# A three-attention transformer kernel: read-out of values and denominators into full rows by VectorE, the key mask carried as a row of the keys' stacks, and other places for the splitting steps

## The reference

```
layer 0:  h = LN(x)*(1+sc)+sh;  q,k,v = h @ qkv_W, rope on halves of 64;  x += g * (softmax(qk/sqrt8, block mask 128x128) v) @ Wo
          h = LN(x)*..+..;      q = h @ cq, k,v = ctx @ ck, cv;          x += g * (softmax(qk/sqrt8, key mask 77) v) @ co
          x += g * (gelu(LN(x)*..+.. @ W1 + b1) @ W2 + b2)
layer 1:  q from LN(x), k,v from LN(ctx), both modulated;               out = x + (softmax(qk/sqrt8) v) @ Wp + bp
```

## Time and profile before

| | us |
|---|---|
| median of 3 runs (1298.3 to 1306.19) | 1305.03 |
| profiled execution | 1309.05 |
| its span, first to last instruction | 1307.3 |
| PE busy | 1182.8 (90%) |
| POOL busy | 898.4 (69%) |
| ACT busy | 887.2 (68%) |
| DVE busy | 736.2 (56%) |
| 16 DMA engines, queue of SP | 44.2% |

### The profile page before, as it was taken

How to read it: one execution, slowest core, us unless ns; L and a number is a source line. 1 busy time by engine, 2 the same in 40 slices (tenths; PEclk the granted TensorE clock), 3 DMA queues, 4 the chain that set the end, 5 groups by cost and what they waited for, 6 DMA issues and landing times.

```text
span 1307.3 us, 42601 instructions
## 1 busy us (share of the span) xinstructions
PE 1182.8 (90%) x16674; PEld 655.9 (50%) x16674; DVE 736.2 (56%) x1613; ACT 887.2 (68%) x1527; POOL 898.4 (69%) x1798
## 2 busy tenths in 40 slices
PE   2778889889888889999999999899998999999998
PEld 1434544444444444555555554344443566666666
DVE  5346677677666665666666664222224666666653
ACT  0235666666666556778778776777876788888765
POOL 0176786786787666777777752556877888888742
PEclk9889899999999899999999998899999899999888
DMA  3475455355354434564554550000023566666650
GB/s 98 117 165 101 74 97 100 71 98 101 69 100 85 85 56 79 84 105 79 88 97 78 97 98 15 1 1 1 4 49 53 85 114 112 117 117 117 109 98 28
DMA packets 147256, 105.84 MB, mean 81 GB/s; under 512 B 25049, under 2 KB 146802, under 8 KB 147058
## 3 DMA queue, kind: packets, MB, share of 16 engines
q1 hardware_dynamic: 147058, 103.12, 44.2%
HBM read 9.08 MB, written 4.19 MB: 10 GB/s over the span
## 4 chain that ended last, share of the span: by engine, by line
PE 59%; POOL 17%; ACT 9%; issue 8%; SPq 2%; DMA 2%; DVE 1%; POOLq 0%; ACTq 0%
PE ps_po L546 10%; PE ps_st L525 6%; PE ps_nat L491 5%; PE ps_pj L438 5%; PE ps_pj L416 4%; PE ps_pj L421 4%; ACT p L798 4%; PE ps_st L558 4%; PE ps_po L567 4%; PE ps_pj L381 4%; PE ps_nat L499 3%; POOL ht L906 3%; POOL ht L901 2%; PE ps_pj L429 2%; POOL ot L862 2%
## 5 line engine op out<-in xcount | busy, mean ns | idle before, releaser
L628 DVE TENSOR_REDUCE negmax<-ps_nat 128x8 f32<-128x616 f32 (+1 forms) x384 | 361.0, 940 | 196.2 <-PE ps_nat L491 109.5
L798 ACT ACTIVATE p<-ps_st 128x1024 f32<-128x1024 f32 (+1 forms) x256 | 260.5, 1018 | 200.5 <-PE ps_st L525 198.3
L546 PE MATMUL ps_po<-p,vz 77*32 77x128 f32 (+1 forms) x6144 | 256.7, 287 | 2.5 <-DVE mt L636 1.1
L862 POOL TENSOR_TENSOR ot<-vv,den 128x256 f32<-128x256 f32 x192 | 139.4, 726 | 150.1 <-ACT den L786 150.0
L798 ACT ACTIVATE p<-ps_st,key_bias 77x1024 f32<-77x1024 f32 x128 | 141.8, 1108 | 70.5 <-PE ps_st L525 70.5
L546 PEld LDWEIGHTS ps_po<-p,vz 77*32 77x32 f32 (+1 forms) x6144 | 149.5, 112 | 41.1 <-issue 4.8
L525 PE MATMUL ps_st<-stacks 64*77 64x128 bf16 (+1 forms) x3072 | 158.3, 224 | 7.6 <-ACT p L798 6.6
L491 PE MATMUL ps_nat<-stacks 64*128 64x77 bf16 (+1 forms) x3072 | 134.9, 210 | 4.8 <-DMA stacks<-parts 3.3
L491 PEld LDWEIGHTS ps_nat<-stacks 64*128 64x128 bf16 x3072 | 78.3, 97 | 116.1 <-issue 101.7
L874 POOL TENSOR_TENSOR whole<-whole,parts 128x512 f32<-128x512 f32 x96 | 98.6, 1027 | 54.4 <-ACT parts L733 54.3
L525 PEld LDWEIGHTS ps_st<-stacks 64*77 64x77 bf16 (+1 forms) x3072 | 104.7, 110 | 49.4 <-issue 28.0
(11 more groups left out here) (138 smaller groups left out, 2144.9 us busy)
## 6 DMA issues: line engine op xcount, KB each, us to landing
stacks<-parts SPq DMA_DIRECT2D x512, 128.0 KB, 3.2
stacks<-parts SPq DMA_DIRECT2D x256, 77.0 KB, 2.6
p<-in_x_dram SPq DMA_DIRECT2D x16, 256.0 KB
out_dram<-part SPq DMA_DIRECT2D x16, 256.0 KB, 2.3
stacks<-mt SPq DMA_DIRECT2D x192, 12.0 KB
p<-in_ctx_dram SPq DMA_DIRECT2D x16, 154.0 KB
stacks<-in_L_xcond_adaLN_W_dram SPq DMA_DIRECT2D x1, 576.0 KB
w<-in_L_xcond_mlp_W_dram SPq DMA_DIRECT2D x2, 256.0 KB
```

What stands on the lines that cost most here:

```text
L546: m = t.matmul(c.ps_po[step % 2][32 * g:32 * g + 32, S * p:S * p + S], c.vz[0:nk, i % 2, step % G, g, at:at + 32], c.p[0:nk, hh, S * g:S * ...
L628: v.tensor_reduce(c.negmax[:, step % 2, :].rearrange("p (h q g) -> p h q g", h=2, q=2)[:, :, p, :], c.nat_pair[:].rearrange("p (h n) -> p ...
L798: a.activation(c.p[0:nk, 2 * p:2 * p + 2, :].rearrange("p h n -> p (h n)"), c.st_pair[0:nk, :], ACT.Exp, bias=bias).then_inc(exped, 1)
L862: p.tensor_tensor(c.ot[:, i % 2, :, S * j:S * j + S], c.vv[:, step % 2, :].rearrange("q (p n) -> q p n", p=2), c.den[:, step % 2, :].rearr ...
```

## The change

1. The value slots of heads are laid so that of each pair of column halves of the bank, one has values where the other has denominators. DVE picks with two 0/1 columns (lower): two tensor_scalar and two scalar_tensor_tensor of 128 columns put all values into vv and all denominators into dd, full rows; the shuffle then runs on dd. ACT, POOL and the output projection work on 128 columns instead of 256, with one product instead of two. wo loses its zero rows and is loaded by 48 DMAs instead of 24, with no wait for a memset.
2. The key mask leaves PE: L499 goes. SP puts the mask of four sequences as one row of every key group into the parts (bring_keys, two DMAs a group), the q stack's matching row is 1 until the maxima overwrite it. The maxima's tile is 128 rows instead of 48, so L942 moves 128 rows of 256 bytes.
3. In the self attention the modulation goes from POOL to ACT (apply_first), and the splitting steps get later slots. "o" and "o2" of groups below 32 share one slot.

```
-            first, second = (LEAD + 17, LEAD + 19) if i < NG - 2 else (LEAD + 16, LEAD + 17)
...
+            if i < 2 * NG:
+                self.add(self.late, b + LEAD + (17 if i < NG - 2 else 16), ("o", i))
+                self.add(self.late, b + LEAD + (17 if i < NG - 2 else 16), ("o2", i))
...
-                    for p in parts:
-                        m = t.matmul(bank[:], wo[:, p, :], c.ot[:, i % 2, p, :], start=p == 0, stop=p == 1)
+                    m = t.matmul(bank[:], c.wo[:, i // NG, :], c.ot[:, i % 2, :], start=True, stop=True)
...
-                    for h in range(2):
-                        kept = c.ps_nat[h][:, 0:4 * nk].rearrange("p (g k) -> p g k", g=4)
-                        t.matmul(kept, c.eye_bf[:, step % B:step % B + 1].broadcast_to([128, S]),
-                                 c.key_rows[:].unsqueeze(1).broadcast_to([128, 4, nk]),
-                                 start=False, stop=True, skip_group_check=True).then_inc(nat_full, 1)
...
-                v.stream_shuffle(c.den[:, step % 2, :], bank[:, 0:2 * S], DEN_ROWS).then_inc(den_here, 1)
-                v.tensor_copy(c.vv[:, step % 2, :], bank[:, 0:2 * S]).then_inc(po_read, 1)
+                v.tensor_scalar(c.dd[:, here, :], second, low, None, ALU.mult).then_inc(picked, 1)
+                v.tensor_scalar(c.vv[:, here, :], second, up, None, ALU.mult).then_inc(picked, 1)
+                dve.wait_ge(picked, 3 * step + 1)
+                v.scalar_tensor_tensor(out=c.dd[:, here, :], in0=first, scalar=up, in1=c.dd[:, here, :], op0=ALU.mult, op1=ALU.add).then_inc(picked, 1)
+                dve.wait_ge(picked, 3 * step + 2)
+                v.scalar_tensor_tensor(out=c.vv[:, here, :], in0=first, scalar=low, in1=c.vv[:, here, :], op0=ALU.mult, op1=ALU.add).then_inc(po_read, 1)
+                dve.wait_ge(picked, 3 * step + 3)
+                v.stream_shuffle(c.den[:, here, :], c.dd[:, here, :], DEN_ROWS).then_inc(den_here, 1)
...
+            def apply_first(i):
+                act.wait_ge(multiplied, plan.norms["n", i] + 1)
+                for b in range(G):
+                    n = G * i + b
+                    part = ht(i)[:, S * b:S * b + S]
+                    m = a.activation(part, part, ACT.Identity, scale=c.mod[:, 1, n:n + 1], bias=c.mod[:, 0, n:n + 1])
+                m.then_inc(applied_first, 1)
...
-            steps = {0: ((3, 0, split_high), (4, 0, split_mid), (5, 1, split_high), (7, 1, split_mid)),
+            steps = {0: ((4, 0, split_high), (6, 0, split_mid), (8, 1, split_high), (9, 1, split_mid)),
-            steps = {0: ((2, 0, turn), (3, 0, take_high), (4, 1, turn), (5, 0, take_mid), (6, 1, take_high), (8, 1, take_mid)),
+            steps = {0: ((2, 0, turn), (4, 1, turn), (5, 0, take_high), (7, 0, take_mid), (9, 1, take_high), (10, 1, take_mid)),
 -            starts = {0: ((6, 0, (0, 1, 2)), (7, 0, (3, 4, 5)), (8, 0, (6, 7)), (9, 1, (0, 1, 2)), (10, 1, (3, 4, 5)), (11, 1, (6, 7))),
+            starts = {0: ((8, 0, (0, 1, 2)), (9, 0, (3, 4, 5)), (10, 0, (6, 7)), (11, 1, (0, 1, 2)), (12, 1, (3, 4, 5)), (13, 1, (6, 7))),
...
-                sp.dma_start(qst[7 * (1 - i % 2):128:24, i % 3, :, S * j:S * j + S], c.mt[:, step % 2, :]).then_inc(max_here[step % 2], 16)
+                sp.dma_start(qst[7 - 6 * (i % 2):128:8, i % 3, :, S * j:S * j + S], c.mt[:, step % 2, :]).then_inc(max_here[step % 2], 16)
...
+            def bring_keys(i):
+                g = i - NG
+                for p in range(2):
+                    sp.wait_ge(stacked[1][p][(i - 1) % 3], 64 * ((i - 1) // 3 + 1))
+                for p in range(2):
+                    sp.dma_start(c.parts[64 * p + 3:64 * p + 64:8, 1, 7, 0:NC], c.key_sets[8 * g:8 * g + 8, :]).then_inc(keyed, 16)
...
-            sp.wait_ge(cleared, 1)
...
-                        load(c.wo[32 * g + 16 * a:32 * g + 16 * a + HD, n, :, :], rows[g, a])
+                        for p in range(2):
+                            load(c.wo[at + HD * p:at + HD * p + HD, n, :], rows[g, a, p])
```

More of the change, by code:

```diff
@@ L29 @@
 SLOTS = 8
-DEN_ROWS = [16 * (r // 16) + HD + r % HD for r in range(32)]
+DEN_ROWS = [r ^ HD for r in range(32)]
 VEC_ROW = {"L0_xcond_adaLN_b": 0, "L1_xcond_bss_q": 9, "L1_xcond_bss_kv": 11, "L0_xcond_norm1_w": 13,
@@ L176, in _ @@
             t.transpose(c.turned_mask[0:SC, S:2 * S], c.key_rows[:], c.eye_bf[:]).then_inc(mask_ps, 1)
+            for b in range(G):
+                m = t.matmul(c.ps_nat[0][:, SC * b:SC * b + SC], c.spread[0:B, b, :], c.key_rows[0:B, :],
+                             start=b == 0, stop=b == G - 1, skip_group_check=True)
+            m.then_inc(mask_ps, 1)
             pe.wait_ge(cond_t, 2)
@@ L232, in __init__ @@
             self.add(self.late, b + (14 if i < NG else 18), ("v", i))
-            first, second = (LEAD + 17, LEAD + 19) if i < NG - 2 else (LEAD + 16, LEAD + 17)
[L234 to L237, removed]
+            if i < 2 * NG:
+                self.add(self.late, b + LEAD + (17 if i < NG - 2 else 16), ("o", i))
+                self.add(self.late, b + LEAD + (17 if i < NG - 2 else 16), ("o2", i))
+            else:
+                self.add(self.late, b + LEAD + (12 if i == GROUPS - 1 else 16), ("o", i))
+                self.add(self.late, b + LEAD + (12 if i == GROUPS - 1 else 17), ("o2", i))
         for g in range(NG):
@@ L265, in __init__ @@
         self.norms = {job[1]: n for n, job in enumerate(j for s, j in order if j[0] == "c")}
+        by_pool = [which for which in self.norms if not self.copied_by_act(which)]
+        self.applied = {which: n + 1 for n, which in enumerate(by_pool)}
         self.dve_jobs, self.act_jobs = {}, {}
@@ L644, in read_out @@
                     dve.wait_ge(mlp_added, NG)
-                v.stream_shuffle(c.den[:, step % 2, :], bank[:, 0:2 * S], DEN_ROWS).then_inc(den_here, 1)
-                v.tensor_copy(c.vv[:, step % 2, :], bank[:, 0:2 * S]).then_inc(po_read, 1)
+                low, up, here = c.lower[:, 0:1], c.lower[:, 1:2], step % 2
+                first, second = bank[:, 0:S], bank[:, S:2 * S]
+                v.tensor_scalar(c.dd[:, here, :], second, low, None, ALU.mult).then_inc(picked, 1)
[6 more added lines that the diff above has]
+                v.stream_shuffle(c.den[:, here, :], c.dd[:, here, :], DEN_ROWS).then_inc(den_here, 1)
             def add_out(i):
@@ L984, in _ @@
                     bring_max(unit_at(slot + 3) // 2)
+                if slot in key_slots:
+                    bring_keys(key_slots[slot])
                 for i, x, t in at_slot.get(slot, []):
```

96 lines of the change are left out of this document (65 added, 31 removed).

## The result

The changed kernel takes 1257.4 us in the median of four runs (1254.2 to 1263.0) against 1303.2 for the kernel before (four runs): a ratio of 0.9657, interval 0.9606 to 0.9707. Forecast was 1236, so the direction and the range held, and a third of the expected gain did not come.

The account below looks back on a forecast made before the run. PE was taken to bound the stages, with a POOL-caused hole in self attention and SP's issuing in setup; SP would bind cross afterwards. Terms +6.5 - 32 - 5 - 28 - 11 = -69.5 gave 1236 us, range 1205 to 1280.

Parts of the forecast that it names:

- Setup: Start of kernel: 48 loads of wo instead of 24 lengthen SP's issuing, +6.5 us, bounds +6.2 to +8.2.
- Read-out: DVE's five operations per step take 1.25 us with overlap, 1.9 with none; 0.6 us extra a step, covered by PE.
- Rival C: DVE's read-out costs its upper price and DVE leads in every stage: 1272 us; chance 0.17.
- Self attention: Group falls from 24.8 to 22.0 us through less PE work, no POOL hole and full clock: -32 us.
- I add 0.7 for what is late next: Self attention group: 0.7 us for slots with late maxima or DVE work, and the k stack.
- Rival D: New slots don't cure POOL's wait, or the late k stack replaces it; self gains only 13 us: 1255; chance 0.11.
- The four groups around the change of stage: Between self and cross attention, clock just under full: lose the 1.1 us product and nothing else, -5 us in all.
- Cross: Cross attention: SP's issues, not PE, end last; group falls from 20.02 to about 18.0 us, -28 us.
- rival E: bring_max's issue grows with its rows to 2.1 us, making cross and layer 1 slower: 1346 us; chance 0.06.
- Layer 1: Halved L387 saves 0.9 us net; group goes from 17.76 to 17.1 us with some misses: -11 us in all.
- The MLP's stretch: The MLP between cross attention and layer 1, some 200 us, has no edited work: no change.
- new short idles: Sign of a wrong prediction: PE's short idles bring the lower clock into cross and layer 1 groups; no size given.

Follow-up runs that it names:

- e4: Changed kernel with the 48 loads of wo issued from ACT's queue instead of SP's; 1247.9 us, ratio 0.9583.
- e8: Changed kernel with two of DVE's five read-out operations left out, so half the values and denominators are missing; ratio 0.9722.
- e11: The kernel of e10 with the k stack's DMAs packed in two SP slots as in e9; 1226.2 us, ratio 0.9431.
- e2: Changed kernel with the self attention's first modulation back on POOL instead of ACT; 1248.5 us, ratio 0.9575.
- e9: Changed kernel with the k stack's eight DMAs in two of SP's slots instead of three; ratio 0.9640.
- e10: Changed kernel with modulation on POOL, wo loads on ACT's queue, and old slots for the last four self attention groups; 1234.9 us, ratio 0.9491.
- e7: Changed kernel with the output product of self and cross attention issued twice; ratio 0.9765.
- e1: Changed kernel with the self attention's splitting steps, turns and DMA starts back in their old slots; 1258.2 us, ratio 0.9661.
- e6: Changed kernel without bring_keys and the wait for it, so cross attention has no key mask; ratio 0.9625.
- e3: Changed kernel with bring_keys issued one slot earlier on SP's queue; 1263.6 us, ratio 0.9702.
- e12: The kernel of e11 with the cross attention's output product issued twice; ratio 0.9410.

## Why the prediction was right in direction and a third too large

**Setup, +6.5, measured +9.2.** The higher end of its bound was right: a halved load costs as much to issue as a whole one (3.71/11 = 0.34), 24 x 0.34 = 8.2, and PE's first product starts 8.1 us later (33.03 for 24.90). The last 1.0 us is within the spread of the column (94.5 to 97.6). e4 shows that it is SP's issuing, and that another queue takes it off the path.

**Read-out, right.** In the changed kernel's timeline:
```profile
283.09 0.34 DVE L661 TENSOR_SCALAR dd<-ps_po,lower 128x128 f32<-128x128 f32 x1
283.35 0.34 DVE L662 TENSOR_SCALAR vv<-ps_po,lower 128x128 f32<-128x128 f32 x1
283.61 0.34 DVE L664 SCALAR_TENSOR_TENSOR dd<-ps_po,lower,dd 128x128 f32<-128x128 f32 x1
283.87 0.34 DVE L666 SCALAR_TENSOR_TENSOR vv<-ps_po,lower,vv 128x128 f32<-128x128 f32 x1
...
284.13 0.30 DVE L668 STREAM_SHUFFLE den<-dd 128x128 f32<-128x128 f32 x1
284.33 1.12 DVE L682 SCALAR_TENSOR_TENSOR xt<-ps_pj,mod,xt 128x128 f32<-128x128 f32 x4
285.37 1.21 DVE L642 TENSOR_REDUCE negmax<-ps_nat 128x8 f32<-128x1024 f32 x1
```
From 283.09 to 284.33 are 1.24 us for the five, forecast 1.25. Rival C is out, by this and by e8. The rule of the Trainium skill ("VectorE: DVE Perf Modes", "The DRAIN you can't avoid") that the forecast set against its rows has an exception in the same section: a next operation that is not held starts earlier. The rows agree with the exception, since operations of 0.34 us start 0.26 apart.

**Self attention, -32, measured -13.7: the step that failed.** PE's work fell as forecast (20.7 busy at full clock), the old hole went, and ten of eleven groups have the full clock. The failed step is "I add 0.7 for what is late next", with the "0.8 to 1.2 us a group" for ACT's modulation ahead of it, taken as hidden: idle time at full clock is 23.61 - 20.70 = 2.9 us a group, not 1.4. What PE waited for between 150 and 370 us, in some nine groups (us in all, times, the longest):
```profile
PE ps_nat L496 <- ACT p L828: 8.7, 17, 0.7
PE ps_po L560 <- ACT p L828: 7.6, 7, 1.1
PE ps_nat L511 <- DMA stacks<-parts: 3.9, 4, 1.5
PE ps_nat L496 <- DVE negmax L642: 2.3, 9, 0.3
```
and the same in e11:
```profile
PE ps_nat L504 <- ACT p L836: 6.6, 10, 0.7
PE ps_po L568 <- DVE mt L658: 4.9, 8, 0.6
PE ps_po L533 <- POOL nm L894: 3.4, 4, 1.7
PE ps_nat L504 <- DVE negmax L650: 2.6, 10, 0.3
```
Two thirds of it are waits for ACT's exponential. The shorter of the masks' two, 0.4 us, comes right behind ACT's modulation, 1.63 us for four, mis-sized and on the path. With the modulation on POOL (e2) it is gone, and so is the values' wait of 1.1 us; PE waits longer for the k stack (5.2 us in all) and for mt, DVE's copy of the turned maxima (4.4), and 0.5 to 0.8 us a group remain as the gain. The masks' other wait, 0.65, stands in a slot in which PE has no product left, since "o2" has moved. The forecast had 0.3 for it and took it for the maxima; this is read from the timeline, no run tests it, and it stays in e11. The maxima themselves (negmax), whose two slots the forecast put at 0.2 each, stop PE for 0.25 a group. In such a slot, the last rows above, DVE has read-out, the addition to x and the maxima one behind the other; shortening the read-out (e8) removes this wait and PE waits longer for the k stack instead. The late k stack is 0.4 a group, and packing it gives some 0.3 (e9, and e11 against e10). With the modulation and the k stack put right the steady group is 22.29 us (e11; 22.66 in the mean of eleven), against the 22.0 of the forecast.

It also follows that the removed product was not worth its 1.1 us: put back, it costs 0.1 to 0.25 (e7), no more than the self column spreads, and with the old slots the changed kernel's self attention takes 295.2 where before took 295.5 (e1). The gain of this stage is that of the slots, 9 to 13.7 us by the executions with the same self attention (281.8 to 286.5).

**Rival D's number.** The measured 1257.4 us and 13.7 in self are nearer to rival D (1255, and 13 in self) than to the forecast. Its mechanism is not what happened: POOL's wait is cured, the late k stack costs 0.4 us a group and no hole as long as the old one, and the gain is the slots' and not the 1.1 of the product. The agreement of the numbers is chance.

**The four groups around the change of stage, -5, measured -0.5.** "Lose the 1.1 and nothing else" was wrong: the new slots cost 9.5 us there (e1), and the timeline has POOL's modulation just ahead of them. I had moved the steps past POOL's list of the steady groups alone.

**Cross, 18.0 a group, measured 18.04: right as a number, partly by chance.** SP's chain was counted as setting each group at 18.0. In fact nine groups of twelve run at 17.27, and three at 20.33 with a lowered clock behind a stop; with no fall the group would be about 17.4 by the numbers above, and with five, as in e9, it is 18.6. The twelve groups and the four after them gave 25.7 us of the 28. That SP's amount of issues counts is shown (e6, some 0.5 a group beside the clock); that their place does, as my count of slots implied, is not (e3). The removed product, counted at 1.1 us, was worth some 0.4 (e7, e12). The timeline has SP's queue close to full:
```profile
603.50 0.60 SPq L985 DMA_DIRECT2D stacks<-mt  x1
604.15 4.44 SPq L1007 DMA_DIRECT2D stacks<-parts  x6
...
615.59 1.32 SPq L992 DMA_DIRECT2D parts<-key_sets  x2
617.01 4.32 SPq L1007 DMA_DIRECT2D stacks<-parts  x6
```
bring_max takes 0.60 here, 0.58 in the median of its 192 issues and 1.91 in the longest (forecast 0.7), so rival E is out. What the removal of L499 is worth by itself was not tried.

**Layer 1, -11, measured -19.1.** The halved L387 gave 0.96 us between full-clock groups (17.67 to 16.71), as worked out net of overlap (0.9). The forecast's 17.1 with misses compares with 16.92 in the mean of eleven. The last three groups gave most of the rest: 49.3 us at a clock of 0.90 in place of 56.7 at 0.82, of which some 5 us are the clock (an estimate, 0.18 x 56.7 less 0.10 x 49.3) and were not foreseen. **The MLP's stretch, 0, measured -4.2** (206.7 to 202.5): with the cross product issued twice it is 204.9 in e7 and in e12, in all other kernels after the change 201.1 to 202.8, so 2 us or more of it are the last cross groups' output products, which fall into it; the rest is open.

**Luck in the sum.** Setup, self, the four groups and cross gave 28 us less than forecast, layer 1 and the MLP's stretch 12 us more. That the miss is no more than a third, and the time inside the range, is partly that these cancel.

The forecast's last sentence named "new short idles" that "bring the lower clock into cross" as what would make it wrong, and put no price on it. It should have had one: three such groups cost about 8 us (3 x 2.8), and runs of one and the same kernel (e4: 1242.0 us at a clock of 0.957, 1255.0 at 0.942) differ by more than many of the edits here.

## What to carry to other kernels

Work taken from an engine that has idle time is paid out only where that engine sets the slot: look slot by slot for what is second, on each engine that gets the moved work, and do it again at the edges of a stage, where the neighbours in the queue are others. Where PE had no idle time and now has some, a late transfer can cost twice, once as the wait and once as the lower clock behind it, and how often it does differs from run to run: compare stages at an equal number of falls. Here each half of a load took as long to issue as the whole had, so cutting loads in two doubled the issue time.

## What was not expected of the hardware

- After 1.75 us without a matmul the granted clock was 0.50 for some 10 us (592.1 to 602.4), and that group took 4.85 us more than the one before it. Other stops of 1.67 and 2.01 us had no fall behind them. Before the change PE was hardly idle in this stage and the clock stayed at 1.00.
- Four 128x128 activations with a scale and a bias for each partition, from and to the same rows, took 1.63 us, each 0.48 long; the four of L769 beside them, out of PSUM, 0.75 in all.
- The maxima's DMA of 32 KB on 128 rows takes 0.60 us to issue where the one of 12 KB on 48 rows took 0.78; it lands 2.3 us after its issue (page of the profile), the stacks of 128 KB 3.2. The Trainium skill ("DMA: Bandwidth & Descriptors", "Why a DMA increments its semaphore by 16 and not by 1") would have them on more engines than before; no row here counts engines or has the landing of before.
